# Expert layer of a graph network: rows gathered over an on-chip slot map, outputs added to the residual in DRAM

## What is computed

```python
logits = flat @ router_w.T                       # flat = _layernorm(x), 3125 x 256, 8 experts
probs = jax.nn.softmax(logits, axis=-1)
topk_probs, topk_idx = jax.lax.top_k(probs, 2)
topk_probs = topk_probs / (jnp.sum(topk_probs, axis=-1, keepdims=True) + 1e-09)
gates = jnp.einsum('nk,nke->ne', topk_probs, onehot)
h = jax.nn.silu(h1) * h3                         # h1, h3: flat times w1[e], w3[e], 256 -> 682
y = jnp.einsum('neh,ech->nec', h, w2)            # 682 -> 256
out = jnp.einsum('ne,nec->nc', gates, y)
x = x + out
```

## Time and profile before

| | |
|---|---|
| median of 3 runs | 2442.72 us |
| the profiled execution's own time | 2447.71 us |
| its span, first to last instruction | 2446.0 us |
| busy: PE, DVE, ACT, POOL | 1842.6, 1503.4, 627.9, 1372.5 us |
| edge aggregation and dense stages | from the start to 950 us |
| routing and expert weights, to the first tile | 950.4 to 1095.4 us |
| expert loop | 1095.4 to 1502 us |
| gather of the expert outputs, projection | 1511.7 to 1610.7 us |
| attention over edges, then the last dense stage | 1610.7 us to the end |

### The profile page before, as it was taken

How to read it: one execution, slowest core, us unless ns; L and a number is a source line. 1 busy time by engine, 2 the same in 40 slices (tenths; PEclk the granted TensorE clock), 3 DMA queues, 4 the chain that set the end, 5 groups by cost and what they waited for, 6 DMA issues and landing times. The chain is left out here.

```text
span 2446.0 us, 37019 instructions
## 1 busy us (share of the span) xinstructions
PE 1842.6 (75%) x9564; PEld 1312.8 (54%) x9565; DVE 1503.4 (61%) x3325; ACT 627.9 (26%) x1252; POOL 1372.5 (56%) x1387
## 2 busy tenths in 40 slices
PE   2879999988997977109999995368888888811687
PEld 2667777763443447106666663256566566601366
DVE  7666644447557867713333333647777777678698
ACT  4000000004546654513333332121111111111342
POOL 3777777762777740464445445847777777632000
PEclk8565555558998987559999998569988989855798
DMA  7333333333002024321111111321111111300100
GB/s 226 105 101 103 105 104 104 105 97 116 1 1 54 1 75 158 97 75 35 37 35 39 37 37 44 89 64 28 28 28 28 28 28 28 27 5 0 26 26 28
DMA packets 113005, 144.03 MB, mean 59 GB/s; under 512 B 46718, under 2 KB 82430, under 8 KB 112822
## 3 DMA queue, kind: packets, MB, share of 16 engines
q0 software_dynamic: 60160, 86.81, 14.8%
q1 hardware_dynamic: 52787, 56.58, 7.7%
HBM read 114.00 MB, written 29.18 MB: 59 GB/s over the span
## 5 line engine op out<-in xcount | busy, mean ns | idle before, releaser
L497 PE MATMUL psA<-oh,G 128*128 128x128 f32 x1568 | 444.9, 448 | 64.0 <-DMA G<-xn_d,gat_i 34.3
L595 POOL DMA_INDIRECT rec_d<-rec,posd x392 | 393.4, 1004 | 167.2 <-issue 124.6
L1500 POOL DMA_INDIRECT g<-tab_d,recs x416 | 395.8, 951 | 148.6 <-issue 126.5
L312 POOL DMA_INDIRECT G<-xn_d,gat_i x392 | 379.5, 968 | 146.4 <-issue 138.8
L497 PEld LDWEIGHTS psA<-oh,G 128*128 128x128 f32 x1568 | 351.2, 312 | 157.5 <-issue 98.3
L1649 PE MATMUL psS<-vv,oh 128*125 128x260 f32 x832 | 290.1, 496 | 92.7 <-DVE acc L1581 92.5
L840 PE MATMUL psZ<-z,W 128*128 (+1 forms) x1344 | 264.1, 359 | 26.0 <-DVE z L739 26.0
L447 DVE TENSOR_TENSOR accT<-accT,psA 128x256 f32 x392 | 165.0, 421 | 170.4 <-PE psA L497 144.3
L1649 PEld LDWEIGHTS psS<-vv,oh 128*125 128x125 f32 x832 | 162.1, 226 | 190.7 <-DVE acc L1581 163.0
L642 ACT ACTIVATE z<-psZ,vec 128x500 f32 (+2 forms) x112 | 70.8, 634 | 643.1 <-PE psZ L833 533.3
L1246 PE MATMUL psH<-we,xh 128*128 x1344 | 215.1, 310 | 0.7 <-issue 0.6
(11 more groups left out here) (257 smaller groups left out, 2760.1 us busy)
## 6 DMA issues: line engine op xcount, KB each, us to landing
raw<-in_L_ffn_w SPq DMA_DIRECT2D x16, 682.0 KB, 10.2
xs_d<-zero SPq DMA_DIRECT2D x1, 7168.0 KB, 23.8
xs<-xs_d SPq DMA_DIRECT2D x56, 128.0 KB, 2.1
y_d<-yv POOLq DMA_DIRECT2D x56, 128.0 KB, 2.0
g<-tab_d,recs POOLq DMA_INDIRECT x416, 2.5
G<-xn_d,gat_i POOLq DMA_INDIRECT x392, 2.7
rec_d<-rec,posd POOLq DMA_INDIRECT x392
raw<-in_L_ffn_w SPq DMA_DIRECT2D x16, 384.0 KB, 10.1
```

The lines of the kernel that those rows point to most:

```text
L312: pool.indirect_dma_start(out=G[:, i, :], out_offset=None, in_=xn_d, in_offset=bass.IndirectOffsetOnAxis(ap=gat_i[:, t:t + 1], axis=0)).th ...
L497: last = nc.tensor.matmul(psA[i // 2][:, i % 2, h, :], G[:, i, 128 * h:128 * (h + 1)], oh[:, i, :], start=True, stop=True)
L595: pool.indirect_dma_start(out=rec_d.rearrange("p (t r) -> (p t) r", r=2), out_offset=bass.IndirectOffsetOnAxis(ap=posd[:, t:t + 1], axis=0 ...
L1500: pool.indirect_dma_start(out=g3[:, n % BODY, j, :], out_offset=None, in_=tab_d, in_offset=bass.IndirectOffsetOnAxis(ap=recs[:, t, 1:2], a ...
```

## The change

- The rows are no longer scattered. POOL stores `xn2` to DRAM (`xn2_d`) chunk by chunk while the router works, in ten transfers, then `x2` (`x2_d`) in two. DVE builds one-hot matrices of the slots, PE multiplies them (50 multiplications into `psM`), and the product is a map from slot to node and gate: `from_i`, `to_i` and `weight`. For each tile POOL gathers 128 rows of `xn2_d` (`fetch`), four tiles ahead, into four buffers.
- The output is scaled with its gate in ACT's copy out of PSUM and added to `x2_d` in DRAM by an indirect transfer with an add (`give`), each issued after the previous one has landed. Empty slots read row 0 and add to 128 spare rows behind the nodes.
- The next stage loads `x2` back in five chunks of two transfers, the first ahead of the projection weights.
- 12 of the 48 weight pieces are split during the router's work, the other 36 after the map; ACT no longer waits for `ex_i`.
- `EDGES_EARLY` goes from 224 to 280, so `PER_TILE` from 3 to 2. PE's loop body covers four tiles, with two more behind the loop. Scratch tiles of the routing lie on `xn2`, so DVE waits for the stores of `xn2`. The zeroing of `xs_d` goes, and so does SP's work in the expert loop. The attention accumulator is cleared by POOL and not by DVE; the store of `tab_d` is split in two.

```diff
-EDGES_EARLY = 224
+EDGES_EARLY = 280
 PER_TILE = (T1 - EDGES_EARLY) // T2
 assert EDGES_EARLY + PER_TILE * T2 == T1
 blk_d = dram("blk_d", (1, T3), I32)
 zero = at("zero", 153 * KB, [128, D])
-xs_d = dram("xs_d", (T2 * 128, D))
-
-s_c2 = [sem(f"s_c2{i}") for i in range(4)]
+xn2_d = dram("xn2_d", (N, D))
+x2_d = dram("x2_d", (N + 128, D))
...
-        sp.dma_start(xs_d.rearrange("(t p) d -> p t d", p=128),
-                     zero[:, :].unsqueeze(1).to_broadcast([128, T2, D])).then_inc(s_zst, 16)
+        sp.dma_start(x2_d[N:N + 128, :], zero[:, :]).then_inc(s_zst, 16)
...
-M = at("M", 57 * KB, [PB, NB * K2, X])
-T = at("T", 57 * KB + 1600, [PB, NB * K2, X])
-top = at("top", 57 * KB + 3200, [PB, NB, X])
-topi = at("topi", 57 * KB + 4000, [PB, NB, X], U32)
+M = at("M", 31 * KB, [PB, NB * K2, X])
...
+XB = 4
+xs = at("xs", o, [128, XB, D]); o += 1024 * XB
...
+    SOON = 12
...
-        sp.wait_ge(s_scx, 16 * NB * K2)
-
-        def load(t, i):
-            sp.dma_start(xs[:, i, :], xs_d[bass.ds(t * 128, 128), :]).then_inc(s_xs[i], 16)
-
-        load(0, 0)
-        load(1, 1)
-        with loop(nc, sp, 0, T2 // 2 - 1) as g:
-            for i in range(2):
-                wait_apart(sp, s_xsT, g * 2 + i + 1, s_tick[3])
-                load(g * 2 + i + 2, i)
...
-        pool.wait_ge(s_slot, 1)
-        for b in range(NB):
-            for k in range(K2):
-                j = b * K2 + k
-                pool.indirect_dma_start(
-                    out=xs_d, out_offset=bass.IndirectOffsetOnAxis(ap=slot_i[:, j:j + 1], axis=0),
-                    in_=xn2[:, b, :], in_offset=None).then_inc(s_scx, 16)
...
+        for c in range(5):
+            cs = slice(5 * c, 5 * c + 5)
+            pool.wait_ge(s_n3, 5 * c + 5)
+            for lo, hi in SPLIT:
+                pool.dma_start(nd[lo:hi, cs, :], xn2[lo:hi, cs, :]).then_inc(s_xn2st, 16)
+        for lo, hi in SPLIT:
+            pool.dma_start(rd[lo:hi, :, :], x2[lo:hi, :, :]).then_inc(s_x2st, 16)
+
+
+        def fetch(t):
+            if t >= XB:
+                pool.wait_ge(s_xsT, t - XB + 1)
+            pool.indirect_dma_start(
+                out=xs[:, t % XB, :], out_offset=None, in_=xn2_d,
+                in_offset=bass.IndirectOffsetOnAxis(ap=from_i[:, t:t + 1], axis=0)).then_inc(s_xs[t % XB], 16)
+
+        def give(t):
+            i = t % 2
             pool.wait_ge(s_yv, 1 + t + 1)
-            pool.dma_start(y_d[t * 128:(t + 1) * 128, :], yv[:, i, :]).then_inc(s_yst[i], 16)
-
+            if t:
+                pool.wait_ge(s_yst[1 - i], 16 * ((t - 1) // 2 + 1))
+            pool.indirect_dma_start(
+                out=x2_d, out_offset=bass.IndirectOffsetOnAxis(ap=to_i[:, t:t + 1], axis=0),
+                in_=yv[:, i, :], in_offset=None, compute_op=ALU.add).then_inc(s_yst[i], 16)
+
+        pool.wait_ge(s_xn2st, 160)
+        pool.wait_ge(s_where, 1)
+        for t in range(XB):
+            fetch(t)
+        pool.wait_ge(s_x2st, 32)
+        pool.wait_ge(s_zst, 16)
         for t in range(T2):
-            store(t, t % 2)
             for j in range(PER_TILE):
                 record(pool, EDGES_EARLY + t * PER_TILE + j)
+            if t + XB < T2:
+                fetch(t + XB)
+            give(t)
...
+                if b >= NB - SOON:
+                    half_w(b - (NB - SOON))
...
-        act.wait_ge(s_ex, 1)
-        for n in range(X * PIECES):
...
+        for n in range(SOON, X * PIECES):
+            half_w(n)
...
+        for n in range(SOON):
+            half_w(n)
+        dve.wait_ge(s_xn2st, 160)
...
+        ids = iota[0:PB, 0:NB]
...
+        for n in range(NB * K2 // JC):
+            js = slice(JC * n, JC * (n + 1))
+            if n >= 2:
+                dve.wait_ge(s_map, n - 1)
+            nc.vector.tensor_tensor(oht[:, n % 2, :, :], iota[0:PB, 0:T2].unsqueeze(1).to_broadcast([PB, JC, T2]),
+                                    place3f[:, 1, js].unsqueeze(2).to_broadcast([PB, JC, T2]), ALU.is_equal).then_inc(s_val, 1)
+            nc.vector.tensor_tensor(ohr[:, n % 2, :, :], iota[0:PB, :].unsqueeze(1).to_broadcast([PB, JC, 128]),
+                                    place3f[:, 0, js].unsqueeze(2).to_broadcast([PB, JC, 128]), ALU.is_equal).then_inc(s_valr, 1)
+            dve.wait_ge(s_val, n + 1)
+            nc.vector.tensor_tensor(valt[:, n % 2, :, :, :], oht[:, n % 2, :, :].unsqueeze(2).to_broadcast([PB, JC, 3, T2]),
+                                    vals[:, js, :].unsqueeze(3).to_broadcast([PB, JC, 3, T2]), ALU.mult).then_inc(s_valr, 1)
+        dve.wait_ge(s_map, NB * K2 // JC)
+        ch.step(nc.vector.tensor_copy(found[:, 0:3, :], psM[:, :, :]))
+        v = found[:, 0, :]
+        ch.step(nc.vector.tensor_tensor(found[:, 1, :], found[:, 1, :], found[:, 2, :], ALU.add))
+        nc.vector.tensor_scalar(weight[:, :], found[:, 1, :], 1.0 / (GS * WS * HS), None, ALU.mult)
+        ch.mark(nc.vector.tensor_scalar(found[:, 2, :], v, 0.0, FOLD, ALU.is_lt, ALU.mult))
+        ch.step(nc.vector.scalar_tensor_tensor(found[:, 3, :], v, -1.0, v, ALU.mult, ALU.max))
+        ch.step(nc.vector.scalar_tensor_tensor(found[:, 3, :], found[:, 3, :], -1.0, found[:, 2, :], ALU.add, ALU.add))
+        ch.step(nc.vector.tensor_scalar(found[:, 2, :], v, 0.0, spare[:, :], ALU.is_equal, ALU.mult))
+        nc.vector.tensor_scalar(from_i[:, :], found[:, 3, :], 0.0, None, ALU.max)
+        ch.step(nc.vector.tensor_tensor(to_i[:, :], found[:, 3, :], found[:, 2, :], ALU.add))
+        dve.sem_inc(s_where, 1)
+        for n in range(SOON, X * PIECES):
+            half_w(n)
...
+        for n in range(NB * K2 // JC):
+            pe.wait_ge(s_valr, 2 * n + 2)
+            for j in range(JC):
+                last = nc.tensor.matmul(psM.rearrange("p s t -> p (s t)"), ohr[:, n % 2, j, :],
+                                        valt[:, n % 2, j, :, :].rearrange("p s t -> p (s t)"),
+                                        start=(n == 0 and j == 0), stop=(n == NB * K2 // JC - 1 and j == JC - 1))
+            last.then_inc(s_map, 1)
...
-        with loop(nc, pe, 0, T2 // 2 - 1) as g:
-            e = experts(g * 2, 3)
-            for i in (1, 0):
-                t = g * 2 + 2 - i
-                turn(t + 1, 1 - i, g + 2)
-                up(t, i, e[2 - i], 0)
-                turn_hidden(t - 1, 1 - i)
-                up(t, i, e[2 - i], 1)
-                down(t - 1, 1 - i, e[1 - i])
+        def tiles(t, loads, n):
+            e = experts(t, n + 1)
+            for j in range(n):
+                i = (j + 1) % 2
+                turn(t + j + 2, (j + 2) % XB, loads + (j + 2) // XB)
+                up(t + j + 1, i, e[j + 1], 0)
+                turn_hidden(t + j, 1 - i)
+                up(t + j + 1, i, e[j + 1], 1)
+                down(t + j, 1 - i, e[j])
+
+        with loop(nc, pe, 0, T2 // XB - 1) as g:
+            tiles(g * XB, g + 1, XB)
+        tiles(T2 - XB, T2 // XB, XB - 2)
...
+        def residual(c):
+            cs = slice(5 * c, 5 * c + 5)
+            for lo, hi in SPLIT:
+                sp.dma_start(x2[lo:hi, cs, :],
+                             x2_d[0:N, :].rearrange("(b p) d -> p b d", p=PB)[lo:hi, cs, :]).then_inc(s_x4[c], 16)
+
+        residual(0)
...
+        for c in range(1, 5):
+            residual(c)
...
-        for j in range(NB * K2):
-            if j >= 8:
-                pool.wait_ge(s_res, j - 7)
-            pool.indirect_dma_start(
-                out=yg[:, j % 8, :], out_offset=None, in_=y_d,
-                in_offset=bass.IndirectOffsetOnAxis(ap=slot_i[:, j:j + 1], axis=0)).then_inc(s_yg[j % 8], 16)
+        nc.gpsimd.memset(acc[:, :, :], 0.0).then_inc(s_a0, 1)
...
-            for j in range(5 * c * K2, 5 * (c + 1) * K2):
-                b, k = j // K2, j % K2
-                dve.wait_ge(s_yg[j % 8], 16 * (j // 8 + 1))
-                dve.wait_ge(s_res, j)
-                nc.vector.scalar_tensor_tensor(x2[:, b, :], yg[:, j % 8, :], gate[:, b, k:k + 1], x2[:, b, :],
-                                               ALU.mult, ALU.add).then_inc(s_res, 1)
-            dve.wait_ge(s_res, 5 * (c + 1) * K2)
+            dve.wait_ge(s_x4[c], 32)
```

More of the change, by code:

```diff
@@ L145, in program @@
         accT = at("accT", 6 * KB, [128, 2, NACC])
-        s_c = [sem(f"s_c{i}") for i in range(4)]
+        s_c = [sem(f"s_c{i}") for i in range(2)]
         W2 = at("W2", 158 * KB, [128, 2, 4, 1024], F16)
@@ L526, in program @@
         zero = at("zero", 153 * KB, [128, D])
-        xs_d = dram("xs_d", (T2 * 128, D))
-        s_c2 = [sem(f"s_c2{i}") for i in range(4)]
+        xn2_d = dram("xn2_d", (N, D))
+        x2_d = dram("x2_d", (N + 128, D))
+        s_c2 = [sem(f"s_c2{i}") for i in range(2)]
         s_off = sem("s_off")
@@ L908, in program @@
         yv = at("yv", o, [128, 2, D]); o += 2048
-        y_d = dram("y_d", (T2 * 128, D))
-        s_c3 = [sem(f"s_c3{i}") for i in range(4)]
+        s_c3 = [sem(f"s_c3{i}") for i in range(2)]
         s_rw = sem("s_rw")
@@ L925, in program @@
         s_tot = sem("s_tot")
```

(27 more changed lines are left out.)

65 lines of the change are left out of this document (46 added, 19 removed).

## The result

The changed kernel took 2360.28 us (median of 4 runs, 2356.41 to 2362.11) against 2443.11 us for the kernel before in the same session (4 runs): ratio 0.9657, 95% interval 0.9641 to 0.9674. Forecast were 2368 us, a range of 2350 to 2398, and faster with 0.94. The profiled execution took 2362.11 us, its span 2360.4; before it was 2447.7.

The account below looks back on a forecast made before the run. Each stretch had its own bound: PE and DVE in the dense stage, POOL's scatters before the first tile, PE in the loop, then the gathers. Terms +13.4 - 23.9 - 13 - 3.5 - 47.9 = -74.9 gave 2368 us, range 2350 to 2398.

Parts of the forecast that it names:

- 56 more records, +13.4: End of dense stage: 56 more POOL records ahead of the barrier start the expert stage at 963.8 instead of 950.4, +13.4 us.
- the cover of 60.8 us: POOL's idle time between its last early record and the expert stage's start, called too short for 56 records taking 73.7 us.
- Router +3.5, stores +1: Expert stage start: twelve weight pieces among the router's work cost +3.5 us, waiting for the stores of xn2 +1 us.
- the first rival: Expert stage start: stores of xn2 land late, shifting the routing by 8 to 25 us, some 2383 us; chance 0.13.
- a share of 27%: DMA before the routing: stores of xn2 get 27%, or 100 GB/s, beside the expert loads; 3.2 MB take 32 us.
- Map, small instructions and pieces: DVE ahead of the first tile: map +25.4 us, small instructions +2.7, 36 weight pieces 33.0 where 48 took 44.0.
- Loop -13: Expert loop on PE: 14 head gaps of 1.02 us go, 14.3 in all, less one microsecond for reading more registers.
- The rival of the dear head: PE's loop head: the doubled body makes 12 heads cost 44 us instead of 26.6, total 2398 us; chance 0.08.
- The third rival: Expert loop: the give's landing paces tiles, a chain deciding from 5.4 us on; a 10 us add gives 2539; chance 0.07.
- End of the loop -3.5: After PE's last tile: the last give replaces three trailing records, so the next stage starts sooner, -3.5 us.
- Projection -47.9: Gather and projection stage: 50 gathers and DVE's 50 additions go, PE paces 25 blocks; 51.0 against 98.9 us, -47.9.
- the warm PE: Projection stage, a rival: PE gets its high clock, 8 us less, 2360 us; inside the forecast case of 0.70.

Follow-up runs that it names:

- the body of eight: PE's expert loop body covers eight tiles instead of four (six passes, straight tail of six), against the changed kernel: 2354.4 us (0.9629 to 0.9656).

## Why the prediction was right, and where it was not

*56 more records, +13.4: mis-sized, +23.6.* They took 79.9 us and not 73.7 (280 records in 378.5 us against 224 in 298.6). The step of 1.317 us came from the last 23 records of before and held none of the long idle times: the one behind the 225th record alone is 5.2 us above the usual 0.30. Behind it the steps are 1.27 us with 24 of 1.4 to 1.5 among them, which makes 5.0 us in all, where 1.317 a step had allowed for 2.5; and the first 224 were 1.6 us faster than before. The barrier came 4.9 us after them instead of 0.4. I had read 0.4 from the end of PE's and DVE's work, the engines that came last before; POOL as the last comer has no row at this barrier. It has one at the end of the loop, 3.77 us behind a record, and that would have been the nearer price. That the cover of 60.8 us is too short was right, and so was the sign.

*Router +3.5, stores +1: right as a sum, wrong between them.* The logits came at 38.7 against 36.2 + 4.5 = 40.7; without the pieces they came at 36.1. So the pieces cost 2.6 and the wait 0. The margin of the stores is 4.9 us, near the first rival: doubling their bytes set it off at 9.3 us in the trace. The price for them had rested on a share of 27%.

*Map, small instructions and pieces.* From the copy of `lg` to the first tile it was 77.6 us, forecast 80.4. Rounds of 3.87 instead of 4.1 make 1.2 of it, and `ex_i` ended 20.9 us after the logits instead of 21.7. The pieces took 32.8 us (1054.6 to 1087.4), forecast 33.0. Here instruction counts times durations of the nearest rows were good to a few per cent.

*Loop -13: the mechanism right, the size -18.5.* The step that was mis-sized is the head: I counted its idle time of 1.02 and then took one microsecond off for more registers. A head costs 1.25 us of period before and 1.07 after, 26 of them against 13: -18.6. (The forecast has 12 left; the straight tail reads its registers too and has the thirteenth.) Part of it is inside the tile behind the head, which takes 6.68 to 6.75 instead of 6.56 us, and no wait shows it. The rival of the dear head is refuted by the body of eight. The Trainium skill's rule ("Runtime: NRT & Kernel Launch", "Instruction fetch mechanics") of a stall at a branch out of the fetched window shows in no head here: the longest is 1.2 us.

*The give sets no pace.* It lands in 3.8 us (read with two buffers; in the changed kernel the trace has no landing for it), under the 5.4 from which a chain would decide. The third rival falls by its price. What the prediction did not see is that POOL's list can close a ring by order alone, without any slow transfer.

*End of the loop -3.5: wrong, +0.6.* I had taken the three records behind the last store as what ends the stage; but the landing and POOL's pause at the barrier count from the last transfer whatever it is. The last give was issued when it should be, its issue ended 2.7 us after PE's last instruction (forecast 2.4); from there to the next stage it was 8.4 us where the forecast had 4.6. A plain scatter needs 6.0 there.

*Projection -47.9: mis-sized, -59.4.* 51.0 was forecast, 39.5 measured. Some 8 us are the warm PE (25 blocks in 21.3 us and not 29), which stood as a rival and was in no sum; the rest are the way in (PE's steps begin 13.4 us after the stage's start and not 15), the upper end that I took for the 25 blocks (1.2), and the way out (1.0). With the clock up, ACT's copies set the pace at two places (0.77 and 1.10 us).

The forecast of the whole was good because the unexpected pauses of POOL (4.5 at the barrier, 4.1 at the loop's end) and the long idle time and dearer steps among the records (6) were about paid for by the loop's heads (5.5), the clock (8) and small terms. That is luck in the sum; the order of the terms was not.

## What to carry to other kernels

Work put on an idle engine is free until its end plus its pause at the barrier reaches the others' end, and from there on each item costs its full step: count items against the cover, here 260 and not 280. A step that is read from twenty items in a row holds no pause that comes once in a hundred: read the whole list. Where one engine issues prefetches and waiting stores in one list, check whether the prefetch stands behind a wait that needs the prefetch; here two more buffers of 1 KB a partition decide between 6.6 and 16.9 us a tile. And price a loop head by the period of its tiles against a tile without a head, not by the idle time before it.

## What the runs showed of the hardware

- POOL reaches a barrier late after an indirect transfer: where POOL comes last, its next instruction comes 3.9 to 4.9 us after the end of the last record. At the loop's end, with the wait for the landing in it, it is 3.8 us after a record, 6.0 after a plain scatter, 7.2 to 8.5 after an adding one, and 9.7 to 10.2 where three records stood right ahead of the add.
- POOL's list of equal records has idle times by count: 1.7 us behind the 113th, 3.8 to 5.7 us behind the 225th, in every kernel that gets that far; every other step, from start to start, is between 1.3 and 2.3 us.
- The first IOTA of the expert stage came 10.1 to 11.4 us after POOL's instruction before it, with nothing to wait for. The Trainium skill ("GPSIMD Engine Reference", "Instruction dispatch") gives some 6 us for the first call of freshly loaded code, with no instruction in the profile; no run here shows whether this is that.
- A direct transfer of 560 rows of 1 KB costs POOL 0.8 us to issue, hardly more than one of 65 rows (0.6), and less than a scatter of 125.
- PE stays at 1.2 GHz through the router, though its rows show it busy without a break from 980 to 995 us (and 29.8 of the 35 us from 975 on); in the projection, where it runs the same kind of blocks at the same pace, it rises to 2.4 GHz. What makes the difference was not tried.
